# Three conditional layers in front of a paged attention: another order of the layers, and the rank-16 products in stacked single-pass matmuls

## The reference

```
x1 = x  + x @ W.T + b + 2 * (x @ lora_A[id0]) @ lora_B[id0]    # rank 16
x2 = x1 + x1 @ weight[id1].T
x3 = x2 + (x2 @ B[id2].T) @ A[id2].T                           # rank 16
out = x3 + attention(x3)      # 32 query heads, 8 key heads of 128, 512 cached keys + 128 new
```

## Time and profile before

| what | value |
|---|---|
| three runs | 1163.53 us median, 1158.74 to 1165.41 |
| the profiled execution, its own time | 1164.61 us |
| its span from the first to the last instruction | 1162.9 us |
| PE busy | 1124.7 us, 97% of the span |
| DVE, ACT, POOL busy | 844.8, 683.1, 475.6 us |
| mean granted TensorE clock | 0.99 of full speed |
| DMA | 277.30 MB moved, 238 GB/s over the span |
| first score matmul of unit 0 | 123.30 us |

### The profile page before, as it was taken

One profiled execution on the slowest core, in us unless ns is written; L12 is line 12 of the kernel. 1 busy time (PEld: TensorE's weight loads), 2 busy tenths in 40 slices (PEclk: granted clock), 3 DMA queues, 4 the chain that ended last, 5 costly groups with the idle time before them and its releaser, 6 DMA issues. The chain is left out here.

```text
span 1162.9 us, 27332 instructions
## 1 busy us (share of the span) xinstructions
PE 1124.7 (97%) x6112; PEld 974.8 (84%) x6112; DVE 844.8 (73%) x2167; ACT 683.1 (59%) x1914; POOL 475.6 (41%) x570
## 2 busy tenths in 40 slices
PE   5999799999999999999999999999999999999996
PEld 3555688898988898988898988898988898988884
DVE  2334677877887877887877887877887877777772
ACT  2223466666666666666666666666666666666661
POOL 6852244443444443444443444443444443333320
PEclk9999799999999999999999999999999999999999
DMA  6673488787887787787787787787787788777774
GB/s 181 190 270 140 151 244 250 236 258 251 256 265 247 239 262 247 253 264 248 238 261 247 255 264 246 238 259 254 251 266 243 238 256 258 229 245 234 239 223 142
DMA packets 125672, 277.30 MB, mean 238 GB/s; under 512 B 13656, under 2 KB 79320, under 8 KB 124634
## 3 DMA queue, kind: packets, MB, share of 16 engines
q1 hardware_dynamic: 78536, 194.28, 47.7%
q10 hardware_dynamic: 35970, 46.15, 16.1%
q0 software_dynamic: 11152, 36.72, 11.4%
HBM read 186.92 MB, written 90.18 MB: 238 GB/s over the span
## 5 line engine op out<-in xcount | busy, mean ns | idle before, releaser
L697 ACT ACTIVATE prob<-prob,low 128x640 f32<-128x640 f32 x256 | 210.1, 826 | 133.0 <-DVE low L1151 133.0
L931 PE MATMUL ps_o<-prob_t,v_raw 128*128 128x256 f32 x1024 | 243.6, 381 | 6.5 <-DMA v_raw<-v_rows_dram,v_row 6.5
L1151 DVE CUSTOM_DVE_ANT_0 prob<-ps_s,mask,q_gain 128x640 f32<-128x640 f32 x256 | 215.6, 879 | 36.7 <-PE ps_s L772 36.7
L931 PEld LDWEIGHTS ps_o<-prob_t,v_raw 128*128 128x128 f32 x1024 | 190.4, 191 | 30.8 <-DMA v_raw<-v_rows_dram,v_row 7.3
L1169 DVE STREAM_TRANSPOSE blocks<-prob 128x640 f32<-128x640 f32 x256 | 207.1, 828 | 2.0 <-ACT prob L702 2.0
L702 ACT ACTIVATE prob<-prob,inv 128x640 f32<-128x640 f32 x256 | 196.7, 816 | 0.6 <-DVE inv L1157 0.6
L770 PE MATMUL ps_s<-kt_hi,qt_hi 128*128 (+1 forms) x512 | 172.1, 336 | 5.3 <-DVE kt_lo L1072 3.8
L870 PE MATMUL ps_q<-w_hi,x_s 128*128 (+1 forms) x512 | 173.0, 398 | 0.0
L772 PE MATMUL ps_s<-kt_hi,qt_lo 128*128 (+1 forms) x512 | 160.5, 314 | 0.0
L771 PE MATMUL ps_s<-kt_lo,qt_hi 128*128 (+1 forms) x512 | 160.3, 313 | 0.0
L650 ACT ACTIVATE ot_hi<-ps_o 128x256 fp32r<-128x256 f32 x128 | 49.1, 384 | 175.7 <-PE ps_o L931 175.7
(11 more groups left out here) (134 smaller groups left out, 2156.6 us busy)
## 6 DMA issues: line engine op xcount, KB each, us to landing
blocks_placed<-blocks SPq DMA_DIRECT2D x128, 640.0 KB, 3.6
prob_t<-blocks_placed ACTq DMA_DIRECT2D x128, 320.0 KB, 5.2
prob_t<-blocks_placed SPq DMA_DIRECT2D x128, 320.0 KB, 6.4
x_s<-xt_split SPq DMA_DIRECT2D x64, 512.0 KB, 3.7
w_raw<-w_qkvo_dram SPq DMA_DIRECT2D x55, 320.0 KB, 3.8
w<-w_t_dram SPq DMA_DIRECT2D x8, 1024.0 KB, 5.2
xt_split<-x3t ACTq DMA_DIRECT2D x8, 512.0 KB, 3.9
w_raw<-w_qkvo_dram POOLq DMA_DIRECT2D x9, 320.0 KB, 4.1
```

Source lines behind the costliest of these rows:

```text
L697: nc.scalar.activation(prob[:, h, :], prob[:, h, :], ACT.Exp, bias=low[:, h:h + 1], scale=-1.0, accum_out=total[:, h:h + 1]).then_inc(exp_ ...
L931: mm = nc.tensor.matmul(ps_o[pair][:, 0:PAIR], v, turned_probs(c, pair), start=c == 0, stop=c == CH - 1)
L1151: nc.vector.tensor_tensor_reduce(out=prob[:, h, :], in0=ps_s[:, score_slot(h):score_slot(h) + KEYS], in1=mask[:, :], scale=q_gain[:, h:h + ...
```

## The change

- **Order on TensorE.** A step now begins with `base(t+1)`, then the turns of x2(t-1), x1(t) and x3(t-2) (before: x3(t-1), at the end of the step), then `lora_in(t+1)`, `layer_2_in(t-1)`, `layer_1(t)`, `layer_2_out(t-1)`, `lora_out(t+1)`. Layer 0 gets two PSUM banks, and the two rank-16 intermediates share one.
- **Stacked rank-16 products.** `h0` and `h2` become `fp32r` tiles of 96 partitions that hold the high part at row 0, the low part at row 32 and the high part again at row 64. The factors `b0` and `a2` are loaded three times into rows 0, 32 and 64, rounded as a whole by ScalarE into `b0_split` and `a2_split`, and their last 32 rows are replaced by the rest on VectorE. One fp32r matmul of 96 rows then gives high·high + low·high + high·low. Per step ScalarE gets two more 16x128 copies and two 96x512 copies; VectorE gets two 16x128 operations and two 32x512 subtractions; SyncE gets four more DMAs. The bias goes into three rows of each slot of `b0` (six DMAs instead of two). Four memsets clear the stacks and two set the rows of ones.
- **Order on VectorE.** The sums now come after all low parts of the step; x1(t+1) comes in front of x3(t-1).
- **Unit 0 beside batch 7.** Unit 0 is projected within step 7 of the layers, behind its three turns. The sines and cosines are made in front of step 5, the query tables in step 5, the key tables in step 6, and unit 0's rotations in step 7, each in front of that step's sums. The load of `x_s` is issued in front of step 6's loads. Steps 2 and 3 are taken out of the loops (on VectorE and ScalarE the whole phase is written out).

```diff
-            b0 = sb("b0", [RANK + 1, 2, HID], scope=p1)
+            b0 = sb("b0", [STACK, 2, HID], scope=p1)
-            h0 = sb("h0", [RANK + 1, P], scope=p1)
+            h0 = sb("h0", [STACK, P], F32R, scope=p1)
...
     # SyncE, first_input; third_adapter likewise with a2
-                        sp.dma_start(b0[0:RANK, at, :], one(lora_b, id0)).then_inc(ab0_in[at], 16)
+                        if not first:
+                            sp.wait_ge(b0_lo_out, e - 1)
+                            sp.nop(nofuse=True)
+                        for row in (HIGH, LOW, AGAIN):
+                            sp.dma_start(b0[row:row + RANK, at, :], one(lora_b, id0)).then_inc(ab0_in[at], 16)
...
     # ScalarE
+                        nc.scalar.activation(h0[HIGH:HIGH + RANK, :], ps_h0, ACT.Copy, scale=LORA_SCALE).then_inc(h0_out, 1)
+                        nc.scalar.activation(h0[AGAIN:AGAIN + RANK, :], ps_h0, ACT.Copy, scale=LORA_SCALE).then_inc(h0_out, 1)
...
                         if t2:
                             second_turned(t - 1, first=second)
+                        first_turned(t, first=first)
+                        if t3:
+                            third_turned(t - 2, first=third)
                         if t2:
                             second_low_rank(t - 1, first=second)
                         if h0_next:
+                            lora_high(t + 1, beside=t if t2 else None)
+                        if t2:
+                            last_factor_high(i, s - 1, first=second)
+                        if h0_next:
+                            first_factor_high(i, s + 1)
                         if input_next:
                             input_high(i, s + 2)
+                        if t3:
+                            store(t - 2)
...
     # TensorE
+                        if l0:
+                            base(t + 1, slot(s + 1), free=None if first else t)
                         if l2:
                             pe.wait_ge(x2_out, t)
                             turn(ps_t2, x2[:, slot(s - 1), :], t2_done)
+                        pe.wait_ge(x1_out, t + 1)
+                        turn(ps_t1, x1[:, slot(s), :], t1_done)
+                        if t3:
+                            third_turn(t - 2, first=third)
+                        if units is not None:
+                            units()
                         if l0:
+                            lora_in(i, s + 1)
                         if l2:
                             layer_2_in(i, s - 1)
+                        layer_1(i, s)
...
                     def layer_2_out(e, at):
-                        pe.wait_ge(h2_out, e + 1)
-                        nc.tensor.matmul(ps_l2[:, :], h2[:, :], a2[:, at, :], start=True, stop=True).then_inc(l2_done, 1)
+                        pe.wait_ge(h2_lo_out, e + 1)
+                        pe.wait_ge(a2_lo_out, e + 1)
+                        nc.tensor.matmul(ps_l2[:, :], h2[:, :], a2_split, start=True, stop=True).then_inc(l2_done, 1)
...
     # VectorE
+                        if t3:
+                            third_turned(t - 2)
                         if input_next:
                             input_low(i, s + 2)
+                        if l0:
+                            lora_low(t + 1)
+                        if l2:
+                            second_low_rank_low(t - 1)
+                        if l2:
+                            last_factor_low(i, s - 1)
+                        if l0:
+                            first_factor_low(i, s + 1)
+                        if between is not None:
+                            between()
+                        second_sum(t, slot(s))
+                        dve.wait_ge(x2_out, t + 1)
+                        if l0:
                             first_sum(i, s + 1)
                         if l2:
+                            third_sum(t - 1, slot(s - 1), first=second)
                             keep_sum(t - 1)
```

More of the change, by code:

```diff
@@ L772, in three, with base @@
                         return nc.tensor.matmul(dst, ll, rh, start=False, stop=final)
-                    def base(e, first=False):
+                    def base(e, at, first=False, free=None):
                         pe.wait_ge(xt_lo_out, e + 1)
+                        if free is not None:
+                            pe.wait_ge(x1_out, free)
                         for k in range(KT):
@@ L839, in layers @@
                             lora_out(t + 1, slot(s + 1))
-                        if l2:
-                            pe.wait_ge(x3_out, t)
-                            if not second:
-                                pe.wait_ge(t3_lo, t - 1)
-                            turn(ps_t3, x3, t3_done)
-                    base(0, first=True)
-                    lora_in(0, 0)
-                    pe.wait_ge(ones_set, 1)
-                    pe.wait_ge(bias_in, 32)
-                    lora_out(0, 0)
-                    pe.wait_ge(ident_in_place, 16)
-                    layers(0, 0, l2=False)
-                    layers(0, 1, second=True)
-                    with pe.Fori(1, B // 2 - 1) as i:
-                        layers(i, 0)
-                        layers(i, 1)
-                    layers(B // 2 - 1, 0)
-                    layers(B // 2 - 1, 1, l0=False)
                     def weight_rows(unit, at, size):
@@ L958, in step, with first_unit @@
                             values(n - 1, first=not out)
-                    pe.wait_ge(w_split, B)
-                    project_queries(0, first=True)
-                    project_new_key(0, first=True)
+                    def first_unit():
+                        pe.wait_ge(w_split, B)
+                        project_queries(0, first=True)
+                        project_new_key(0, first=True)
+                    base(0, 0, first=True)
+                    lora_in(0, 0)
+                    lora_out(0, 0)
+                    pe.wait_ge(ident_in_place, 16)
+                    layers(0, 0, l2=False, t3=False, first=True)
+                    layers(0, 1, t3=False)
+                    layers(1, 0, third=True)
+                    layers(1, 1)
+                    with pe.Fori(2, B // 2 - 1) as i:
+                        layers(i, 0)
+                        layers(i, 1)
+                    layers(B // 2 - 1, 0)
+                    layers(B // 2 - 1, 1, l0=False, units=first_unit)
+                    turn_cached(0, ps_s[:, 0:512])
+                    turn_rotated(0)
                     pe.wait_ge(x2_out, B)
                     turn(ps_t2, x2[:, slot(B - 1), :], t2_done)
-                    turn_cached(0)
+                    third_turn(B - 2)
                     layer_2_in(B // 2 - 1, 1)
                     layer_2_out(B - 1, slot(B - 1))
-                    turn_rotated(0)
-                    pe.wait_ge(x3_out, B)
-                    pe.wait_ge(t3_lo, B - 1)
-                    turn(ps_t3, x3, t3_done)
+                    third_turn(B - 1)
                     step(0, False, out=False, pv=False)
@@ L1049, in _ @@
                         rest(w0_lo[:, k, :], w0_raw[:, k, :], w0_hi[:, k, :]).then_inc(w0_lo_out, 1)
+                    first_factor_low(0, 0)
+                    lora_low(0)
                     first_sum(0, 0)
```

216 lines of the change are left out of this document (128 added, 88 removed).

## The result

| | before | after |
|---|---|---|
| median of 15 runs each | 1163.0 us (1158.74 to 1168.02) | 1171.43 us (1166.23 to 1181.73) |
| ratio | | 1.0071 [1.0052, 1.0090] |
| profiled execution, span | 1164.61, 1162.9 | 1172.93, 1171.2 |
| first score matmul | 123.30 | 130.92 |
| from there to the end | 1039.6 | 1040.3 |

The change makes the kernel 0.7% slower, where 1161.7 us was forecast. The attention kept its length, so the loss is the 7.6 us by which the scores start later (of the two executions profiled).

A forecast was written before the change was run, and what follows sets the result against it. TensorE was taken to bound the layers' phase; with steps at 11.7 us against 11.75, scores start at 121.5 instead of 123.3 and the attention is unchanged: 1163.53 - 1.8 = 1161.7 us, range 1156.0 to 1167.0.

The forecast's parts named there:

- With both, a step is 11.1 + 0.2 + 0.35 = 11.7 us: Layers' step: 11.1 us with the low-part chain, plus 0.2 for partition changes and 0.35 for contention, against 11.75 before.
- Four small copies at 0.17: ScalarE's four rank-16 copies at the head of the low-part chain, 0.17 us each, from 6.25 to 6.93 after base's start.
- TensorE's own step 10.27: TensorE's work per layers' step falls from 11.74 to 10.27 us, as two two-pass matmuls become single-pass at 0.24 each.
- Who releases `layer_2_out`: In each step, low parts made by VectorE behind ScalarE release it, after about 0.9 to 1.4 us of TensorE idle.
- Contention 0.35 a step: Three VectorE subtractions with both inputs in SBUF slow beside GpSimd: 0.35 us a step, bounds none and 1.6.
- Partition changes: VectorE outputs starting at rows 32 and 64 don't overlap neighbours: none to 0.27 us a step, taken as 0.2.
- The start: Memsets and extra bias DMAs are hidden; base(1) stays at 20.95 us and base(2) starts at 30.4 instead of 32.05.
- Step 7's tables: VectorE's key tables stand before x2(6)'s sum without cover, so step 7's turns take 3.3 us; cost about 1.9.
- the rival with 15%: Clock falls at unit 0's projection after step 7's idle: 3.1 us more, 1164.8 us; chance 15%.
- The junction: From the projection's end at 106.25 us through unit 0's rotations and batch 7's last layer, scores start at 121.5.
- Contention takes over: Rival: GpSimd slows all three subtractions every step, 12.9 us a step, 1167.9 us; sign turns at 12.1; chance 11%.
- The chain is hidden: Rival: ScalarE and VectorE keep up, steps 1 to 5 take 10.27 us, 7.0 us more gained, 1154.7 us; chance 11%.

The follow-up runs named there:

- experiment 4: The change with GpSimd's two-input subtraction for the first nine weight chunks replaced by a plain copy; 1168.5 us, 1.0041 of the kernel before the change.
- experiment 3: The change with six filler fp32r matmuls put in front of `layer_2_out` on TensorE in steps 1 to 6; 1167.63 us, 1.0033 of the kernel before the change.
- experiment 6: The change without the stack: rank-16 products in two-pass float32 as before, new order kept; 1161.79 us, 0.9976 of the kernel before the change.
- experiment 7: The change with factors' parts early, `input_low` behind the small low parts, and tables behind the sums; 1156.54 us, 0.9931 of the kernel before the change.
- experiment 5: The change with query and key tables behind the sums of steps 5 and 6 on VectorE; 1169.21 us, 1.0052 of the kernel before the change.
- experiment 2: The change with both factors' rounding and rests moved to the step's beginning on ScalarE and VectorE; 1155.09 us, 0.9912 of the kernel before the change.

## Why the prediction was wrong

Its stretches, against the profile after (us):

| stretch | forecast | measured | |
|---|---|---|---|
| start to base(2) | 30.4 | 29.48 | -0.9 |
| base(2) to base(7) | 58.0 | 64.45 | +6.45 |
| base(7) to the end of step 7's turns | 13.6 | 16.54 | +2.9 |
| projection | 4.25 | 4.70 | +0.45 |
| to the end of `layer_2_out` | 4.85 | 4.75 | -0.1 |
| to `turn_rotated` | 2.9 | 3.44 | +0.5 |
| from there to the scores | 7.5 | 7.56 | +0.1 |

Together +9.4, of the 9.7 by which the median missed.

**The step that failed** is "With both, a step is 11.1 + 0.2 + 0.35 = 11.7 us", and it failed twice.

First, a term of its sum was mis-sized. "Four small copies at 0.17" took 1.16 us, not 0.68: the 0.17 is from two copies with outputs at the same row, these have theirs at rows 0 and 64 by turns. This is 0.48 us in every step. The rest of the chain was near: factor copies 1.06 for 1.00, the partition changes on VectorE 0.25 for 0.2, some 0.2 between a low part's end, its matmul and the next base. With `xbt_lo` at 0.75 a step is 12.02, where the same terms gave 11.35: 5 x 0.67 = 3.35 us. Experiment 4 shows this alone, 11.95.

Second, a term was missing. The wait inside a step was costed at its own length, and none of the sum or the rivals let it take the clock with it. Bases that ran at 1.2 GHz took 1.56, 0.96 and 1.63 us more (4.34, 3.74 and 4.41 from base to turn against 2.78), the two rank-16 products 0.25. In steps 3 and 4 that is 2.8 us, in step 6 another 1.7 with what stands right in front of its base; at step 7's turns 0.7 and at the projection 0.4, by experiment 4, where the same wait had no fall. Of the miss of 9.4 us this is 5.6. That the falls come from the waits is shown by experiments 3, 6 and 7: with the waits filled or gone, the clock stays up through the steps. Each of these is one trace, but the mean granted clock of all executions agrees: its median is 0.985 in the change, 0.990 before and in experiments 3 and 6, and in the change's slowest execution (1181.73 us) it is 0.977, in its fastest (1166.23) 0.990. What decides that one wait of 1.33 us is followed by a fall (92.95) and another (40.09) isn't, I can't say; in experiment 4 four of five such waits had none.

Point by point:
- *TensorE's own step 10.27*: right and a little high; 9.98 in experiment 7. The stacked matmuls are 0.47 us long, not 0.24 to 0.32, but the distance from `lora_out` to the next base is 0.31, and 0.23 in experiment 7, so the cost was near.
- *Who releases `layer_2_out`*: right, VectorE's factor rest, with 1.33 to 1.39 idle in front (forecast 0.9 to 1.4).
- *Contention 0.35 a step*: right in the mean by luck, wrong in its shape. Two of five `xbt_lo` were long, by 1.25 and 0.80 us, 0.41 a step; the chain's other subtractions weren't. The Trainium skill's row on SBUF interfaces (page "GPSIMD Engine Reference"), that GpSimd contends with VectorE's instructions with two SBUF inputs, agrees: `xbt_lo` is 0.69 always once GpSimd has one input. GpSimd's copies aren't free of it, though: `w_hi` took 1.20 beside one in experiment 4.
- *Partition changes*: a full-size low part and the next are 0.72 apart across such a change (75.98 to 76.70 in experiment 4), 0.61 without (51.28 to 51.89). That agrees with the rule that the prediction cites from the Trainium skill (page "VectorE: DVE Perf Modes").
- *The start*: memsets end at 3.88, in front of the low part at 4.32, as forecast. The six bias DMAs with SyncE's stall take 5.66 us from 3.66, so that batch 0's adapter is issued at 10.39 in place of 4.61; `lora_in` at 16.16 doesn't wait for it. It came out 0.9 us better, since base(1) ran at the full clock. The 4.12 us of base(1) before were read as a clock "still rising"; by the windows it is 1.00 from 12 to 20 us, and 0.52 from 20 to 22. With base(2) at 25.8 and 29.4 for the same code (experiments 3 and 5), the nearness of 30.4 is luck.
- *Step 7's tables*: forecast 1.9 of wait; 2.3 found, from 105.67 to 107.99. That it would also bring the clock down was the rival with 15%. It did in the profiled execution, at a lower price (0.7 + 0.4, for 3.1), and in experiment 4 it didn't.
- *The junction*: right to 0.6 us, and the attention to 0.7. Its clock was taken between the two levels; it was 1.00 until 128 and then 0.50.
- *Contention takes over* put the point of decision at 12.1 us a step. Steps averaged 12.9, and the kernel is slower, but mostly for the other two reasons.
- *The chain is hidden* held for no kernel in the change's order. With the factors early it is what happens in most steps, and it gives 1155.09 where the rival said 1154.7. That they are so near is luck: the profile there still has waits of 2.22 and 4.27 us where the rival had none and 1.9.

## What to carry to other kernels

A pass saved on the busiest engine is worth nothing if its operands go through two other queues in the same step: take out of that chain whatever depends on loads alone, which here turned 0.7% slower into 0.9% faster with the same instructions. Price a wait within a saturated TensorE phase not by its length alone: here four of six waits of 1.3 to 2.6 us cost 1.1 to 1.7 us more in what followed. And when such a wait is removed, look for the next queue that comes late (here a load, GpSimd's last chunk, the tables): repairs on top of experiment 2 were expected to bring up to 8 us more and brought nothing that the medians can tell. Compare stretches from a point behind the start, since the start alone moved by several us from one execution to the next.

## What was not expected of the hardware

- ScalarE copies of 16x128 start 0.15 to 0.18 us apart with outputs at the same row, and 0.29 apart, their whole length, when each output starts 64 rows from the last. These are different kernels and the output types differ too (float32 and `fp32r`); since a copy to `fp32r` at row 0 is followed by another at row 0 after 0.16 us in the change itself, the row is the likeliest cause, though no run changes it alone.
- One VectorE subtraction of two SBUF operands took from 0.69 to 2.00 us beside GpSimd's two-operand one of 1.53 us: it was delayed by 1.31 us of those 1.53. A one-operand copy of VectorE's (`y<-x` at 69.74) took 1.71 in place of 0.43 beside another of these, and a subtraction took 1.20 in place of 0.68 beside GpSimd's copies (experiment 4).
- The granted clock fell to 0.50 behind some waits and stayed at 1.00 behind others of the same length. In the change and the experiments together, up to step 7, it fell behind 5 of 15 waits of 1.32 to 1.39 us, behind 4 of 6 of 2.18 to 2.64, and in or behind all 5 of 3.27 to 4.27.
